# A gated product ahead of the scaling of o, and the v projection and its copy moved back in TensorE's and ScalarE's orders

## The reference, cut to what matters

```
for i in range(DEPTH):        # 6
    x = attn_layer(shift_tokens(x), Wqkv[i], q_scale[i], k_scale[i], Wo[i]) + x
    x = ffn_layer(shift_tokens(x), ln_g[i], ln_b[i], W1[i], b1[i], W2[i], b2[i]) + x
# attn_layer: q, k, v = split(x @ Wqkv) in 16 heads of 64; q, k normalised, scaled, turned (rotary);
#             windows of 32 tokens see themselves and the window before; softmax; @ v; @ Wo
# ffn_layer:  xn = layer norm of x;  a, gate = split(xn @ W1 + b1);  (a * gelu(gate)) @ W2 + b2
```

## Time and profile before

| | us |
|---|---|
| median of 3 runs | 1879.38 (1878.95 to 1880.2) |
| the profiled execution | 1880.17 |
| its span, first to last instruction | 1878.4 |
| PE busy | 1770.3 (94%) |
| DVE busy | 1610.7 (86%) |
| POOL busy | 1499.3 (80%) |
| ACT busy | 1326.8 (71%) |
| granted TensorE clock, share of full | 0.98 |

### The profile page before, as it was taken

The page is one execution under the profiler, slowest core; times in us unless marked ns, Lnnn a source line. Parts: engine busy times, 40 slices in busy tenths (PEclk is TensorE's granted clock), DMA queues, the critical chain, the costliest instruction groups (busy, mean ns, idle before and its releaser), DMA issues.

```text
span 1878.4 us, 48610 instructions
## 1 busy us (share of the span) xinstructions
PE 1770.3 (94%) x18100; PEld 1124.5 (60%) x18100; DVE 1610.7 (86%) x2780; ACT 1326.8 (71%) x2363; POOL 1499.3 (80%) x1200
## 2 busy tenths in 40 slices
PE   6689999999999999999999999999999999999986
PEld 4446655665666656666656666656666666566563
DVE  3499989989989899889899889898998998998873
ACT  2367777777777687777777777777777777877763
POOL 2299978888888888888888888888888888888760
PEclk8689999999999999999999999999999999999998
DMA  3013222223222223222222222222222222222221
GB/s 105 8 42 86 73 61 66 64 53 83 71 68 67 60 56 84 63 70 72 55 58 74 73 73 60 65 61 73 70 79 56 68 62 55 57 72 55 54 60 31
DMA packets 154989, 120.46 MB, mean 64 GB/s; under 512 B 42577, under 2 KB 151173, under 8 KB 154629
## 3 DMA queue, kind: packets, MB, share of 16 engines
q1 hardware_dynamic: 154757, 117.35, 24.2%
HBM read 18.66 MB, written 1.05 MB: 10 GB/s over the span
## 4 chain that ended last, share of the span: by engine, by line
PE 80%; DVE 9%; POOL 4%; issue 3%; SPq 1%; DMA 1%; ACT 1%; DVEq 0%; POOLq 0%; ACTq 0%
PE qk_bank L367 16%; PE ring_bank L437 10%; PE ring_bank L461 8%; PE ring_bank L378 8%; PE sc_bank L412 8%; PE ring_bank L505 7%; PE ring_bank L425 5%; PE ring_bank L388 4%; PE ring_bank L399 3%; PE ring_bank L450 3%; PE ring_bank L516 3%; POOL turned L1033 1%; POOL turned L1040 1%; DVE o L884 1%; DVE rn L828 1%
## 5 line engine op out<-in xcount | busy, mean ns | idle before, releaser
L1033 POOL TENSOR_TENSOR turned<-qkn,tables 128x512 f32<-128x512 f32 x384 | 489.7, 1275 | 230.4 <-DVE qkn L836 218.1
L1040 POOL TENSOR_TENSOR turned<-qkn,tables 128x512 f32<-128x512 f32 x384 | 499.2, 1300 | 0.0
L367 PE MATMUL qk_bank<-wqkv,xT 128*128 128x512 f32 x768 | 367.8, 602 | 6.9 <-DVE qkn L844 6.4
L619 ACT ACTIVATE vs<-ring_bank 128x512 f32<-128x512 f32 x192 | 114.6, 597 | 215.8 <-PE ring_bank L378 201.7
L1069 POOL TENSOR_TENSOR turned<-turned 128x512 f32<-128x512 f32 x192 | 254.0, 1323 | 15.0
L1076 POOL TENSOR_TENSOR turned<-turned 128x512 f32<-128x512 f32 x192 | 244.8, 1275 | 15.1
L378 PE MATMUL ring_bank<-wqkv,xT 128*128 128x512 f32 x384 | 216.5, 646 | 36.1 <-DVE uT L942 34.6
L437 PEld LDWEIGHTS ring_bank<-vw,pT 128*32 128x32 f32 x6144 | 156.8, 110 | 144.6 <-issue 144.5
L646 ACT ACTIVATE kB<-ring_bank 64x512 f32<-64x512 f32 x384 | 225.4, 587 | 23.2 <-PE ring_bank L399 20.9
L810 DVE TENSOR_REDUCE ss<-sq 128x16 f32<-128x1024 f32 x192 | 232.0, 1208 | 8.1 <-ACT sq L610 8.1
L884 DVE TENSOR_TENSOR o<-ring_bank,rr 128x512 f32<-128x512 f32 x192 | 132.3, 689 | 124.1 <-PE ring_bank L437 122.5
(11 more groups left out here) (156 smaller groups left out, 3142.0 us busy)
## 6 DMA issues: line engine op xcount, KB each, us to landing
vw<-vs SPq DMA_DIRECT2D x1152, 64.0 KB, 2.1
vw<-vs SPq DMA_DIRECT2D x672, 32.0 KB, 1.9
wqkv<-in_L_ffn_Wqkv_dram SPq DMA_DIRECT2D x20, 384.0 KB, 3.5
wo<-in_L_ffn_Wo_dram SPq DMA_DIRECT2D x20, 128.0 KB, 3.3
w<-in_L_ffn_W_dram SPq DMA_DIRECT2D x6, 341.0 KB, 3.3
wqkv<-in_L_ffn_Wqkv_dram SPq DMA_DIRECT2D x1, 1536.0 KB, 10.2
x<-in_x_dram SPq DMA_DIRECT2D x2, 512.0 KB, 4.2
out_dram<-x SPq DMA_DIRECT2D x4, 256.0 KB, 2.3
```

Source lines behind the costliest of these rows:

```text
L367: mm = pe.matmul(QK[u % 2][:, i * UW:(i + 1) * UW], tok, wqkv[:, layer % 2, cut:cut + UW], start=True, stop=True)
L1033: return pool.tensor_tensor(heads(turned[:, u % 2, 2 * i, :]), heads(qkn[:, u % 2, i * UW:(i + 1) * UW]), table.unsqueeze(1).to_broadcast( ...
L1040: return pool.tensor_tensor(halves(turned[:, u % 2, 2 * i + 1, :]), halves(qkn[:, u % 2, i * UW:(i + 1) * UW])[:, :, ::-1, :], table.rearr ...
```

## The change

Three pieces of code move; no instruction is added or taken away. TensorE's v projection goes behind the scores, ScalarE's copy of v goes behind copy_oT and squares, and VectorE's gated product of block 0 goes ahead of scale_o. As the banks are handed out in program order, the turns of a slot become pv, o, v, p, k, extra, q. (In the diff, context is cut.)

```
@@ TensorE
                 queries_keys(n)
                 attend(n - 5)
-                values(n)
                 transpose_o(n - 6)
                 scores(n - 3)
+                values(n)
                 transpose_p(n - 4)
@@ ScalarE
-                copy_v(n)
                 copy_oT(n - 6)
                 squares(n)
+                copy_v(n)
                 copy_pT(n - 4)
@@ VectorE
                 if s == 7:
                     add_attention(g - 1, 1)
+                if s == 4:
+                    gated(g - 2, 0)
                 scale_o(n - 5)
                 if s == 3:
                     layer_norm(g - 2)
-                if s == 4:
-                    gated(g - 2, 0)
```

## The result

The changed kernel takes 1858.34 us (median of 4 runs, 1857.93 to 1858.73) against 1879.16 us before (4 runs): a ratio of 0.9888 (95% interval 0.9871 to 0.9905), 20.8 us less. The forecast was 1856. The profiled execution took 1857.99 us, its span is 1856.0, and the spans differ by 22.4 us.

What follows compares the result with a forecast made beforehand. TensorE, busy 1770.3 of 1878.4 us, was taken as the bound. 1880.2 - 36.1 (stall) + 12.5 (late loads) = 1856.6, forecast as 1856 us because the profiled execution was 0.8 above the median; own range 1851 to 1860.

Steps and rivals of the forecast that it cites:

- The stall and its size: In slot 4, v's wait for the gated product costs 1.64 us a group; removing it gains 36.1 us.
- TensorE's neighbours: On TensorE, o, scores, v and p in the new order sum to 3.08 us as before; taken as 0.
- The new wait: The extra product waits for v's later copy, its load 0.14 us late; 12.5 us over slots 4 to 7.
- The sum: Whole kernel: 1880.2 - 36.1 + 12.5 = 1856.6, forecast as 1856 us.
- The reading that the rows overruled: TensorE pulls weight loads ahead, hiding the extra product's 0.14 us lateness; 1844 us. Profile rows said it is paid.
- VectorE behind the stall: After slot 4's stall goes, scale_q comes about 1.2 us earlier, leaving 0.2 to 0.35 us slack; cost taken as 0.
- a slot 6 that begins with a wait for scale_q: Sign set beforehand in the profile after: if slot 6 begins so, (b) is right.
- (b): Rival: VectorE bounds the freed stretch, or slots 1 to 3 pay too; 1858 to 1868 us, chance 0.15.
- That slots 1 to 3 would absorb TensorE's delay: In slots 1 to 3 TensorE's 0.14 us disappears in its waits; taken as nothing, otherwise up to 9 us more.
- (a): Rival: the extra product doesn't pay for v's late copy; 1844 us, chance 0.22.
- (c): Rival: on ScalarE, squares stay late and hold up v's copy, load 0.55 us late; 1893 us, chance 0.03.
- (d): Rival: o still waits in slot 4 because the gated product isn't early; 1893 us, chance 0.02.

Runs made afterwards that it cites:

- e1: The kernel before with only the gated product moved ahead of scale_o, TensorE's and ScalarE's orders unmoved: 1861.98 us, ratio 0.9892.
- e2: The changed kernel with the gated product put back behind scale_o, leaving only the two moved orders: 1879.31 us, ratio 0.9990.
- e12: e1 with the four small VectorE operations' second operand read from PSUM, normalisation of q and k not computed: 1821.63 us, ratio 0.9698.
- e5: The changed kernel with the clamp's and newton's second operand read from PSUM, normalisation of q and k not computed: 1838.09 us, ratio 0.9773.
- e3: The changed kernel with the v projection ahead of the scores but still behind o: 1855.69 us, ratio 0.9861.
- e6: The changed kernel with sum_p moved between newton's second and third operation: 1893.06 us, ratio 1.0065.

## Why the prediction was right, and where it wasn't

**The stall and its size: right.** Slot 4 lost 33.0 us in 22 groups, and the prediction's two terms for it are 36.1 - 22 x 0.14 = 33.0. e1 has 7.55 us there to the hundredth, and e2 shows the whole 34.6 us of wait again once the gated product is back.

**TensorE's neighbours: right.** o, scores, v and p take from 962.17 to 965.26, 3.09 us, where the prediction had 3.08.

**The new wait: right as a delay, wrong as a price.** The copy of v ends 6.24 us behind the start of the slot and the load comes at 6.29; the forecast had 6.23 and 6.29. That is 0.14 us late in each of the six slots, and the matmuls behind it follow by 0.14 (slot 4 7.69 for 7.55, slot 7 9.43 for 9.27). The sum had 12.5 us for it. But e1, which has none of it, has the same period as the changed kernel. In this kernel its cost is nothing that can be seen; e12 against e5 shows that it is 16 us where nothing hides it. The reading that the rows overruled, that such a delay is hidden, stays overruled by e12.

**VectorE behind the stall: the part that failed.** The prediction said that the scale_q for which slot 6 waits would come 1.2 us earlier and leave 0.2 to 0.35 us of room, with 0 to 3 us as bounds, and took 0. It came 0.39 us earlier: 974.98 - 959.28 = 15.70 us behind the start of slot 4, where it was 915.87 - 899.78 = 16.09. TensorE was ready at 15.4. The prediction treated VectorE's stretch as work of a fixed length that moves as a whole. Up to scale_o it moved even further: the forecast had VectorE 0.3 to 0.45 us late there, and it was idle for 0.29 us ahead of 970.03. Its stretch from scale_o to scale_o took 970.03 - 0.29 - 962.34 = 7.40 us and not 8.0. Behind scale_o it could not: GpSimd's sum of q ends 14.27 us behind the start of slot 4 with the stall or without it (14.25), and newton's third operation was held until then. In slot 4 the 0.6 us that the moved gated product set free went the same way: newton's first operation began earlier and ended with the same GpSimd operation (0.94 us for 0.26). The prediction had seen one such hold, in the clamp, and allowed 0.15 us for it; slots 5 and 6 lost 0.47 us a group beside TensorE's own lengths in e5, some three times as much. By the prediction's own sign, a slot 6 that begins with a wait for scale_q, this is rival (b).

**The sum: 1856 came out near 1858.3 by luck in good part.** For slots 4 to 7 the prediction had -36.1 + 12.5 = -23.6 us. The trace has -33.0 + 9.6 + 5.0 + 3.3 = -15.1. The 8.5 us of difference lie in slots 5 and 6 and are what the holds cost. They were made up by 7.7 us for which the sum had no term: 3.5 in slots 0 to 3, 1.5 ahead of them, and 2.7 from the start of the run, which wanders. The 12.5 us were right as what the load's delay does to slots 4, 6 and 7, but they were not the price of the moved orders, as e1 shows: the period is 71.6 us a group with them or without. What sets it is a path over VectorE's held operations and GpSimd's rotation. e5 shows this, as the period falls to 70.76 us once the holds are gone. In slots 3 to 5 the path was followed above; through the rest of the group it was not followed link by link.

That slots 1 to 3 would absorb TensorE's delay was right, and e2 shows that it goes for the whole group. The layer's first groups, where a bias product lengthens slot 2, do not share this period: the six of them take 2.9 us less in e3 than in the changed kernel, which is the larger part of the 4.5 us that e3 gains between slots 2 and 191. The cause was not followed.

**The rivals.** (a) is out: the loads were late and delayed the matmuls. (b) came true in its sign, and 1858.3 lies at the lower edge of its range as well as inside the forecast's own. (c) did not occur: squares ended at 964.37, 0.55 us before the copy of v began. (d) did not occur.

What stays open: a version of newton with an operand in PSUM that computes the right values was not tried, as all eight banks are in use.

## What to carry to other kernels

When a stall is taken out of the busiest engine, look for the loop that its idle time had been feeding. Here three kernels with different TensorE work took 71.6 us a group, and equal sums over pairs of slots showed the other bound before its cause was known. A delay on the critical engine is worth nothing while another loop is slower, so price it again in a kernel in which that loop is gone. And a small operation whose duration ranges from 0.17 to 1.2 us may be a wait in disguise: compare its end with the ends of GpSimd's operations.

## What the runs showed of the hardware that I had not expected

- A VectorE operation on 128x16 fp32 elements takes 161 to 171 ns with one of its operands in PSUM and 405 to 557 ns on average with both in SBUF beside a busy GpSimd; held ones end 0.03 to 0.04 us behind the GpSimd operation. The section on the chip says that the engines meet only at semaphores; these two also meet here, where no semaphore stands between them.
- tensor_scalar with a constant and a single SBUF operand is held as much as tensor_tensor with two (554 and 557 ns), while tensor_reduce keeps its time (0.67 to 0.69 us on 128x512, 1.20 to 1.22 on 128x1024), and so do scale_q and scale_k, which read PSUM and SBUF (0.68 and 0.69 us).
- A small operation that starts 0.01 to 0.02 us ahead of the next GpSimd operation passes (44 of 44 in the changed kernel), and one that starts 0.10 to 0.14 us behind its start is held for all of it (95 of 95 in e6). Splitting newton by a 0.67 us reduction turned the first case into the second, and cost 35 us in the kernel.
